# First MLP layer of a graph-attention kernel: one full-width float32 product against three two-part products, inputs split a step early, segment sums moved one step later

## What is computed

```python
wk = relu(edge_features @ k_w1 + k_b1) @ k_w2 + k_b2      # "hidden" is the relu
wv = relu(edge_features @ v_w1 + v_b1) @ v_w2 + v_b2
k  = sum_s sh[:, s] * (x_dst @ Cqk[:, s]) * wk            # tensor product, s = 0..8
v  = sum_s sh[:, s] * (x_dst @ Cv[:, s]) * wv
attn = sum over d of q[edge_src] * k                      # per head
out = segment softmax of attn, weighted segment sum of v, then W_out, norm
```

## Time and profile before

| | |
|---|---|
| median of 3 runs | 5025.04 us (5020.54 to 5040.35) |
| profiled execution | 5049.76 us, span of its instructions 5047.8 us |
| first and last chunk's transposes (L797) start | 78.1 and 4620.5 us |
| busy share of the span | PE 95%, PEld 89%, DVE 80%, ACT 68%, POOL 74% |
| granted TensorE clock, mean over the span | 0.975 |

### The profile page before, as it was taken

One profiled execution on the slowest core, in us unless ns is written; L12 is line 12 of the kernel. 1 busy time (PEld: TensorE's weight loads), 2 busy tenths in 40 slices (PEclk: granted clock), 3 DMA queues, 4 the chain that ended last, 5 costly groups with the idle time before them and its releaser, 6 DMA issues. The chain is left out here.

```text
span 5047.8 us, 115383 instructions
## 1 busy us (share of the span) xinstructions
PE 4772.7 (95%) x35582; PEld 4503.5 (89%) x35582; DVE 4058.6 (80%) x5044; ACT 3414.7 (68%) x6495; POOL 3713.3 (74%) x3494
## 2 busy tenths in 40 slices
PE   7999999999999999999999999999999999998256
PEld 6999999999999999999999999999999999998143
DVE  5888888888888888888888888888888888886435
ACT  2677677677777767767777677777777777776137
POOL 3777777777777777777777777777777777774460
PEclk9999999999999999999999999999999999998578
DMA  8899999999999999999999999999999999996220
GB/s 218 202 215 210 208 210 214 208 214 210 212 207 214 213 208 213 211 210 211 211 213 211 207 216 213 216 214 214 213 216 212 214 214 216 212 213 158 91 68 26
DMA packets 693458, 1006.45 MB, mean 199 GB/s; under 512 B 120054, under 2 KB 378168, under 8 KB 693160
## 3 DMA queue, kind: packets, MB, share of 16 engines
q1 hardware_dynamic: 574856, 753.93, 65.7%
q0 software_dynamic: 112960, 242.16, 22.7%
q10 hardware_dynamic: 5600, 9.83, 0.7%
HBM read 826.64 MB, written 178.93 MB: 199 GB/s over the span
## 5 line engine op out<-in xcount | busy, mean ns | idle before, releaser
L825 PE MATMUL psum<-chi,zhi 128*128 128x256 f32 x7840 | 2316.9, 301 | 2.2 <-DVE rv L731 2.1
L535 POOL DMA_INDIRECT gq<-qtab,idxs x1568 | 1881.1, 1200 | 478.0 <-issue 475.8
L828 PE MATMUL psum<-clo,zhi 128*128 128x256 f32 x7840 | 2144.4, 282 | 0.0
L530 POOL DMA_INDIRECT gx<-in_xg,idxs x1568 | 1555.4, 992 | 465.0 <-issue 453.5
L827 PE MATMUL psum<-chi,zlo 128*128 128x256 f32 x6272 | 1768.4, 282 | 0.0
L825 PEld LDWEIGHTS psum<-chi,zhi 128*128 128x128 f32 x7840 | 1478.6, 189 | 99.3 <-issue 99.3
L828 PEld LDWEIGHTS psum<-clo,zhi 128*128 128x128 f32 x7840 | 1476.2, 188 | 0.0
L827 PEld LDWEIGHTS psum<-chi,zlo 128*128 128x128 f32 x6272 | 1183.6, 189 | 93.0 <-issue 93.0
L685 DVE TENSOR_TENSOR z<-psum,shb 128x1536 f32<-128x1536 f32 (+1 forms) x784 | 1130.5, 1483 | 126.2 <-PE psum L797 118.7
L580 ACT ACTIVATE zhi<-z 128x1536 fp32r<-128x1536 f32 (+1 forms) x784 | 993.5, 1267 | 247.9 <-DVE z L685 244.0
L710 DVE TENSOR_TENSOR zlo<-z,zhi 128x1536 fp32r<-128x1536 f32 (+1 forms) x784 | 922.2, 1217 | 0.0
(11 more groups left out here) (210 smaller groups left out, 6335.1 us busy)
## 6 DMA issues: line engine op xcount, KB each, us to landing
shb<-in_shT SPq DMA_DIRECT2D x392, 640.0 KB
shb<-in_shT SPq DMA_DIRECT2D x392, 512.0 KB
rows<-ot SPq DMA_DIRECT2D x392, 416.0 KB
e<-in_eT SPq DMA_DIRECT2D x392, 128.0 KB
drow<-rankd SPq DMA_DIRECT2D x392, 128.0 KB
gx<-in_xg,idxs POOLq DMA_INDIRECT x1568
gq<-qtab,idxs POOLq DMA_INDIRECT x1568
qtab<-qs ACTq DMA_DIRECT2D x25, 256.0 KB, 5.7
```

What stands on the lines that cost most here:

```text
L530: nc.gpsimd.indirect_dma_start(out=gx[:, s, k, :], out_offset=None, in_=xg[:, :], in_offset=bass.IndirectOffsetOnAxis(ap=ids[:, k:k + 1], ...
L535: nc.gpsimd.indirect_dma_start(out=gq[:, s, k, :], out_offset=None, in_=qtab[:, :], in_offset=bass.IndirectOffsetOnAxis(ap=ids[:, TC + k:T ...
L825: mm(tpb[:, k, :], zhi[:, s, j, e], chi[:, j, :], start=(j == 0), stop=False)
L828: last = mm(tpb[:, k, :], zhi[:, s, j, e], clo[:, j, :], start=False, stop=(j == ST - 1))
```

## The change

The first layer's weights `w1` are split into `w1hi` and `w1lo` in the preparation, and each pair's edge features into `e2hi` (ACT, `features_first_part`) and `e2lo` (DVE, `features_rest`); `hidden` becomes three float32r products that accumulate in one bank. The split for the next pair is made in the step of the current pair's second chunk. The segment sums move from chunk `t - 6` to chunk `t - 7` and, on TensorE, to the front of the step: first half, `turned_x`, `hidden`, second half. On ACT the order changes with it, and `segments` makes the `seg` of chunk `b` itself. The run of steps is one longer. One mask tile in place of two is loaded, some tiles are placed differently in SBUF, and the last stage counts on three semaphores where it had one for each name.

```diff
-    for n in range(R0 + UN * TURNS, NC + LAG + 2):
+    for n in range(R0 + UN * TURNS, NC + LAG + 3):
...
+                    v.tensor_copy(w1hi[:, :, :], w1[:, :, :]).then_inc(w_split, 1)
...
+                    v.tensor_tensor(w1lo[:, :, :], w1[:, :, :], w1hi[:, :, :].bitcast(fp32), ALU.subtract)
...
-                            sp.wait_ge(h_full, c.value() - 2)
+                            sp.wait_ge(e2lo_done, c.turn(2) - 1)
...
-                        for ahead, tile in ((0, nmf), (1, nmb)):
-                            src = newd[bass.ds(g.value() * CH + ahead, GT * P)].rearrange("(t e) -> t e", t=GT)
-                            sp.dma_start(tile[:, s, :], src.unsqueeze(1).broadcast_to([GT, H, P])).then_inc(nm_in[s], 16)
+                        src = newd[bass.ds(g.value() * CH, GT * P)].rearrange("(t e) -> t e", t=GT)
+                        sp.dma_start(nmf[:, s, 0:P], src.unsqueeze(1).broadcast_to([GT, H, P])).then_inc(nm_in[s], 16)
...
-                        if (t + (-LAG - 1)).there():
-                            store(t + (-LAG - 1))
+                        if (t + (-LAG - 2)).there():
+                            store(t + (-LAG - 2))
...
+                    def features_first_part(c):
+                        act.wait_ge(e_in[c.r // 2 % 2], 32 * (c.turn(4) + 1))
+                        if c.old(2):
+                            act.wait_ge(h_full, c.value())
+                        f(e2hi[:, :], e2[:, c.r // 2 % 2, :], ACT.Copy).then_inc(e2hi_done, 1)
```

ACT's step:

```diff
                     def step(t, find, fetch, count):
-                        c, b = t + 1, t + (-LAG)
+                        c, b, a = t + 1, t + (-LAG), t + (-LAG - 1)
+                        if a.there():
+                            sums(a, 0)
+                        if t.there():
+                            edge_weights(t)
                         if b.there():
                             weights(b)
-                        if t.there():
-                            edge_weights(t)
+                        if c.there():
+                            hidden(c)
+                        if a.there():
+                            sums(a, 1)
+                            maxima(a)
+                        if (c + 1).there() and c.r % 2 == 1:
+                            features_first_part(c + 1)
                         if c.there():
                             z_first_part(c, 0)
-                            hidden(c)
+                            hidden_first_part(c)
                             z_first_part(c, 1)
-                            hidden_first_part(c)
                             if c.r % 2 == 1:
                                 feature_rows(c + (-1))
                         if b.there():
-                            sums(b, 0)
-                            maxima(b)
-                        if (b + 1).there():
-                            segments(b + 1)
-                        if b.there():
-                            sums(b, 1)
+                            segments(b)
```

DVE's part, then `hidden` and the step of TensorE:

```diff
+                    def features_rest(c):
+                        dve.wait_ge(e2hi_done, c.turn(2) + 1)
+                        if c.old(2):
+                            dve.wait_ge(h_full, c.value())
+                        v.tensor_tensor(e2lo[:, :], e2[:, c.r // 2 % 2, :], e2hi[:, :].bitcast(fp32), ALU.subtract).then_inc(e2lo_done, 1)
...
                             hidden_rest(c)
+                        if (c + 1).there() and c.r % 2 == 1:
+                            features_rest(c + 1)
+                        if c.there():
                             z_rest(c)
...
-                        mm(hbank, w1[:, c.r % 2, :], e2[:, s, :], start=True, stop=True).then_inc(h_full, 1)
+                        k = c.r % 2
+                        mm(hbank, w1hi[:, k, :], e2hi[:, :], start=True, stop=False)
+                        mm(hbank, w1hi[:, k, :], e2lo[:, :], start=False, stop=False)
+                        mm(hbank, w1lo[:, k, :], e2hi[:, :], start=False, stop=True).then_inc(h_full, 1)
...
                     def step(t, find, fetch, count):
-                        c, b = t + 1, t + (-LAG)
+                        c, a = t + 1, t + (-LAG - 1)
+                        if a.there():
+                            sums(a, 0)
                         if c.there():
                             turned_x(c)
                             hidden(c)
+                        if a.there():
+                            sums(a, 1)
                         if t.there():
                             tensor_products(t)
                         if c.there() and c.r % 2 == 1:
                             turned_features(c + (-1))
-                        if b.there():
-                            sums(b, 0)
                         if c.there():
                             edge_weights(c)
-                        if b.there():
-                            sums(b, 1)
```

More of the change, by code:

```diff
@@ L151, in gnn_kernel, with eb @@
         banks = [psum[:, i * 512:(i + 1) * 512] for i in range(8)]
+        edges = ctx.enter_context(ExitStack())
+        def eb(name, shape, dt=fp32):
+            return edges.enter_context(nc.sbuf_tensor(name, shape, dt))
+        chi = eb("chi", [P, ST, KV], f32r)
+        clo = eb("clo", [P, ST, KV], f32r)
+        w1hi = eb("w1hi", [P, 2, P], f32r)
+        w1lo = eb("w1lo", [P, 2, P], f32r)
+        b1c = eb("b1c", [P, 1])
+        w2hi = eb("w2hi", [P, KV], f32r)
+        w2lo = eb("w2lo", [P, KV], f32r)
+        b2hl = eb("b2hl", [P, KV], f32r)
+        ones = eb("ones", [P, P], f32r)
+        idx_all = eb("idx_all", [P, 2 * EC], i32)
+        ndcol = eb("ndcol", [P, EC])
         load = sem("load")
@@ L783, in _ @@
                     v.memset(shb[D:P, :, ST - 1, :], 0.0).then_inc(shb_zero, 1)
-                    dve.wait_ge(shb_zero, 1)
+                    v.memset(nmf[:, :, P:P + 1], -BIG).then_inc(shb_zero, 1)
+                    dve.wait_ge(shb_zero, 2)
+                    features_rest(Chunk(0, 0))
                     steps(dve, step)
@@ L885, in _ @@
                     steps(pe, step)
+        edges.close()
         with ExitStack() as mend:
@@ L1085, in gnn_kernel @@
             st_d, st_a, st_pe = sem("stats_dve"), sem("stats_act"), sem("stats_pe")
-            SS = {k: sem(f"{k}_made") for k in ("r", "y", "dd", "sq", "lg", "rs", "x1", "s0", "h0", "h1", "y2", "dd2", "sq2",
-                                                "lg2", "rs2", "o")}
-            prod_made = sem("products_made")
-            PRODUCTS = ("mean", "var", "z0", "z1", "z2", "mean2", "var2")
+            MADE = {"pe": ("mean", "var", "z0", "z1", "z2", "mean2", "var2"),
+                    "act": ("r", "sq", "lg", "rs", "h0", "h1", "sq2", "lg2", "rs2"),
+                    "dve": ("y", "dd", "x1", "s0", "y2", "dd2", "o")}
+            made_by = {e: sem(f"blocks_made_by_{e}") for e in MADE}
             def wait_made(engine, name, i, j):
-                if name in PRODUCTS:
-                    engine.wait_ge(prod_made, (i * len(PRODUCTS) + PRODUCTS.index(name)) * GN + (j + 1))
-                else:
-                    engine.wait_ge(SS[name], i * GN + (j + 1))
+                for e, names in MADE.items():
+                    if name in names:
+                        engine.wait_ge(made_by[e], (i * len(names) + names.index(name)) * GN + (j + 1))
             with ExitStack() as fin1:
@@ L1293, in product @@
                                 wait_made(pe, after, i, j)
-                                t.matmul(bank_of(j), lhsT[:, :], W(src, j), start=True, stop=True).then_inc(prod_made, 1)
+                                t.matmul(bank_of(j), lhsT[:, :], W(src, j), start=True, stop=True).then_inc(made_by["pe"], 1)
                         def turn(i):
@@ L1333, in turn @@
                                 if past(i):
[L1334 to L1335 removed]
+                                    wait_made(act, "o", i + (-1), GN - 1)
+                                f(W("r", j), xp[:, ncols(i, j)], ACT.Identity, bias=st[:, 9:10]).then_inc(made_by["act"], 1)
                             for j in range(GN):
```

56 lines of the change are left out of this document (22 added, 34 removed).

## The result

The changed kernel takes **6191.54 us** (median of 4 runs, 6179.89 to 6195.95), the kernel before 5022.79 us beside it: ratio 1.232, 95% interval 1.228 to 1.235. The forecast was 5148 us with 5080 to 5205. The sign was right, and the size was missed by more than 1,000 us.

The account below looks back on a forecast made before the run. TensorE bounds the kernel, with POOL's gathers close beside it. Terms -71 + 212 - 28 + 12 = +125 on the profiled 5049.8 us give 5175, carried to plain runs 5150, stated as 5148 us; range 5080 to 5205.

Parts of the forecast that it names:

- The step that failed: SP: SP's queue: `targets` waits for a later `seg`, with masks, `store` and `harmonics` behind it; priced at 0.
- The split on ACT and DVE: 0.6 us on ACT and 0.69 on DVE every second step, said to lie in idle time: 0.
- the gathers become slower: Rival: DVE's `features_rest` slows POOL's gathers to 12.03 us a step; 5197 us, chance 0.13.
- the gathers hold the whole stage: Rival: the `seg` chain doesn't bite and POOL's 11.68 us a step sets the main stage; 5060 us, chance 0.07.
- The profile that I said one would see: Main stage: TensorE idle about 1 us for `seg` every second step; 11.9 us a step, in pairs of 11.1 and 12.7.
- The sums at the front: TensorE's `sums(a, 0)` waits for ACT's `seg` in even-`t` steps: 1.1 us in 193 steps, +212 us (183 to 241).
- The first layer: TensorE's `hidden` as three float32r products: 0.86 us to 0.68, 0.18 a step, -71 us (-55 to -84).
- The gathers: TensorE, at 11.90 us a step, gets slower than POOL's 11.68, so waits for node rows go: -28 us (or 0).
- The end: The emptying steps get about 1 us longer over seven steps, plus one more step: +12 us (0 to 15).
- the term that was to decide: The wait of TensorE's sums at the front of the step for ACT's `seg`: +212 us.

Follow-up runs that it names:

- after_padded: The changed kernel with only 64 idle waiting instructions added ahead of ACT's main loop: 6169.2 us, ratio 1.225 to the kernel before.
- store_first_padded: The changed kernel with SP's store at the head of its step, before the wait for `seg`, and 64 idle instructions ahead of ACT's loop: 5140.9 us.
- store_first: The changed kernel with SP issuing the store at the head of its step, before it waits for `seg`: 5301.1 us, ratio 1.053.
- split_alone: The kernel before, its old order of TensorE, ACT and SP's store kept, with the three-product first layer and the two splits: 5183.3 us, ratio 1.031.
- seg_earlier_padded: The changed kernel with ACT making `seg` of chunk `b + 1`, not `b`, and 64 idle instructions ahead of ACT's loop: 5061.5 us, ratio 1.006.
- move_seg_early: The changed kernel with the first layer as one float32 product, no split, and ACT making `seg` of chunk `b + 1`: 5001.7 us, ratio 0.994.
- split_padded: The kernel before, old order kept, with the three-product first layer, its splits and 64 idle instructions ahead of ACT's loop: 5003.9 us, ratio 0.9946.

## Why the prediction was wrong

**The step that failed: SP.** "`targets` now waits for a `seg` made a step later, and behind it in SP's queue are the masks (one issue fewer), `store` and the next `harmonics`. [...] I price it at 0 and keep it for the upper end." The `store` was named as queued behind the wait, but I followed only the `harmonics` to their reader. The reader of a *finished store* is whoever writes its buffer next, ACT's `sums(a, 0)`, which the same change had made the first operation of ACT's step, one step later than the sums. With two slots there is no step of slack between them. It measured 1,028 us (`after_padded` to `store_first_padded`), 890 with the reload in both.

**The clock.** The sum has no term for it. In the changed kernel 676 us of the stage ran at 1.2 GHz, against 10 before, 126 in `store_first` and 0 in `store_first_padded`. TensorE stood still for 860 us of the stage, at 417 places, before the sums, at 168 of them for over 3 us. I read this as a part of the ring's cost and not a cause of its own, since it came and went with the idle time; no run changes the one without the other.

**"The split on ACT and DVE": 0.** As far as work beside other work goes, it was nearly right: in the old order TensorE waits 53 us more for `keys and values`, which `features_rest` pushes back. What no row of before could show is what a few more instructions ahead of ACT's loop and in it (268 and 297 before, 281 and 303 in `split_alone`) do to the loading of that loop. It cost 22 us behind the ring and 160 to 179 us in the three others that were measured both ways. The rival "the gathers become slower" gave the wrong reason: taking VectorE's part away gives 15 of the 60 us between `seg_earlier_padded` and `move_seg_early`. The milder one, "the gathers hold the whole stage" at 11.68 us a step and 5060 us, is what came in `seg_earlier_padded`, where the chain through `seg` is cut: 11.67 and 5061.5.

**What held.** In `store_first_padded`, where only the forecast's own terms are left:

- The profile that I said one would see: steps "in pairs of about 11.1 and 12.7". They are 10.98, 12.62, 11.09 and 12.74.
- The sums at the front: 1.1 us in 193 steps, 212 us (183 to 241). In the stage it is 184 us in 192 steps, 0.96 us each, the low end. The two rows of waits, 162.0 + 37.4 = 199 us, are of the whole span; 16 us of them stand behind the last chunk's `turned_x`.
- The first layer: 0.86 us to 0.68. The first product starts 0.36 us behind the transposes and the sums 0.78 us behind it (3002.07 to 3002.85). In `move_seg_early`, with the float32 product in the same place, these are 0.44 and 0.86: 0.16 a step, 63 us of the 71. By the account of the stage it is 0.17 (11.52 to 11.35), 67 us.
- The gathers: -28 us. The wait went from 43.5 us to 20.5, -23.
- The end: +12 (0 to 15). From the last chunk's `turned_x` to the end of the span it is 428.9 us against 427.6, +1, the term that was sized worst.

Together -67 + 184 - 23 + 1, and -5 for the half clock that is gone (10 us of it before), make +90, and the two profiled executions, from which all these rows come, are 90 us apart (5139.8 and 5049.8). The forecast for them was +125. It was 35 us too high, 28 of them on the sums at the front and 11 on the end, the other terms 4 to 5 us each to one side or the other. The medians are further apart, 5140.9 - 5026.8 (before in that comparison) = +114, since the plain runs of before scatter from 5014 to 5076 with a median 23 us below its profiled one, and those of `store_first_padded` do not (5140 to 5144, profiled 5139.8). The prediction took 25 us off for that difference, and the changed kernel didn't have it. So the 7 us are two errors that nearly cancel. The mechanism of the term that was to decide is right, and its size is right to 15%; the model of who waits for whom stopped one engine short, and the range, 5080 to 5205, was built of the terms that I had, with nothing for a ring that wasn't seen. (One reading was off without consequence: VectorE is busy 846 of 1,000 us, not 847.)

**What beats both kernels.** The split in the old order, with ACT's loop in its place (`split_padded`, 5003.9 us, 0.9946), or the move with the segment matrix a step early and no split (`move_seg_early`, 5001.7 us, 0.9937, 0.988 to 0.999). Both are about half a per cent.

## What to carry to other kernels

When a wait in a queue of transfers becomes younger, follow every transfer behind it to its *second* reader, the engine that needs the buffer back, and ask whether the path from there leads to the event waited for. If it does, it is a ring, and its length is the step: add it up before any other term. And look at the instruction queue of the page before believing any small difference between two kernels with loops: if its packets jump from tens to hundreds, compare again with some idle instructions ahead of the loop.

## What the runs showed of the hardware

- An engine's loop can lose 3 to 5 us at each turn, with some 231 more packets in the instruction queue over 47 turns, by where the loop starts: 24 idle instructions ahead of an unchanged loop of 297 made 47 turns cost 145 us (5026.3 to 5171.5).
- A store of 416 KB lands 3.8 us after its issue (median of 392 in the page of the changed kernel; 3.45 in the step shown).
- With 168 pauses of TensorE of over 3 us (860 us of pauses before the sums in all), 676 us of a stage of 5,659 ran at the half clock, 1.2 GHz; with pauses of 1 us in 192 steps of `store_first_padded`, none.
- Three float32r products of 512 columns (0.32 us behind the first, 0.23 behind the others) take 0.16 us less than one float32 product of that size by the starts in the same place of the step, and 0.18 by the account of the stage (11.52 to 11.34 a step in `split_padded`).
